# A fused transformer block's attention: one more merging transfer and one more addition in place of two raw chunks, a ring of nine slots, and the batch loop written out

## The reference, cut to what matters

```python
x = x + 0.5 * ffn(layernorm(x))
x = x + attn(layernorm(x))
x = x + 0.5 * ffn(layernorm(x))

def attn(x, Uq, Vq, bq, Uk, Vk, bk, Uv, Vv, bv):      # H = 8 heads of 32 columns
    q, k, v = lowrank(x, Uq, Vq, bq), lowrank(x, Uk, Vk, bk), lowrank(x, Uv, Vv, bv)
    scores = einsum('bqhd,bkhd->bhqk', q, k) / 32 ** 0.5
    out = einsum('bhqk,bkhd->bqhd', softmax(scores), v)
```

## Time and profile before

| | us |
|---|---|
| median of 3 runs | 4593.1 (4589.04 to 4593.98) |
| the profiled execution | 4578.01, with a span of 4576.3 |
| ACT, exponentials of scores (L1674) | 2256.0 busy, 4096 of them |
| POOL, additions to a running sum (L1537) | 1771.0 busy, 633.5 idle before them |
| PE, scores (L1795) | 1535.0 busy, 4096 of them |
| merging transfers (L1514) | 384 of 1024 KB, 8.4 from issue to landing |

### The profile page before, as it was taken

How to read it: one execution, slowest core, us unless ns; L and a number is a source line. 1 busy time by engine, 2 the same in 40 slices (tenths; PEclk the granted TensorE clock), 3 DMA queues, 4 the chain that set the end, 5 groups by cost and what they waited for, 6 DMA issues and landing times. The chain is left out here.

```text
span 4576.3 us, 72040 instructions
## 1 busy us (share of the span) xinstructions
PE 3734.0 (82%) x21202; PEld 1454.5 (32%) x21202; DVE 3267.3 (71%) x4504; ACT 3214.1 (70%) x6587; POOL 2553.1 (56%) x966
## 2 busy tenths in 40 slices
PE   0177683899999999999999999999999999920276
PEld 0144452233333333333333333333333333300143
DVE  8644675887777777777777777777777777648544
ACT  5043572788888888878888887888888888834043
POOL 0011001477777777767777777777777777753111
PEclk9988896899999999999999999999999999965588
DMA  8200899577877878778777887788788788678100
GB/s 276 77 3 4 293 392 293 106 158 160 174 168 164 170 169 179 158 159 173 166 162 166 174 177 153 171 168 176 160 177 168 158 175 166 129 226 300 37 5 5
DMA packets 326047, 743.31 MB, mean 162 GB/s; under 512 B 26060, under 2 KB 209888, under 8 KB 270112
## 3 DMA queue, kind: packets, MB, share of 16 engines
q0 software_dynamic: 57216, 407.92, 44.8%
q1 hardware_dynamic: 222496, 284.46, 20.9%
q10 hardware_dynamic: 45952, 46.27, 2.9%
HBM read 198.90 MB, written 136.48 MB: 73 GB/s over the span
## 5 line engine op out<-in xcount | busy, mean ns | idle before, releaser
L1674 ACT ACTIVATE at_probs<-at_ps_s 128x512 f32<-128x512 f32 x4096 | 2256.0, 613 | 345.6 <-PE at_ps_s L1795 261.6
L1559 DVE TENSOR_REDUCE at_part_max<-at_ps_max 128x3 f32<-128x1536 f32 x1024 | 1801.0, 1759 | 472.4 <-PE at_ps_max L1708 464.5
L1537 POOL TENSOR_TENSOR at_pool_sum<-at_pool_sum,at_probs 128x2048 f32<-128x2048 f32 x384 | 1771.0, 4612 | 633.5 <-DMA at_probs<-at_probs 632.4
L1795 PE MATMUL at_ps_s<-at_qs,at_ks 97*128 97x512 f32 (+1 forms) x4096 | 1535.0, 453 | 37.2 <-ACT at_probs L1674 22.5
L1742 PE MATMUL at_ps_acc<-at_probs,at_v 128*32 128x512 f32 x8192 | 1099.2, 609 | 0.9 <-ACT at_probs L1674 0.9
L1795 PEld LDWEIGHTS at_ps_s<-at_qs,at_ks 97*128 97x128 f32 (+1 forms) x4096 | 630.4, 189 | 1149.2 <-ACT at_probs L1674 823.0
L1561 DVE TENSOR_REDUCE at_part_max<-at_max_copy 128x1 f32<-128x512 f32 x1024 | 691.7, 676 | 0.0
L1623 ACT COPY at_max_copy<-at_ps_max 128x512 f32<-128x512 f32 x1024 | 610.1, 596 | 102.1 <-PE at_ps_max L1708 101.8
L1708 PE MATMUL at_ps_max<-at_ks,at_qs 32*128 32x512 f32 x4096 | 526.0, 501 | 82.5 <-DMA at_ks<-qk_parts 48.8
L1514 POOL DMA_DIRECT2D at_probs<-at_probs x384 | 346.9, 903 | 209.1 <-PE at_ps_acc L1742 201.3
L1708 PEld LDWEIGHTS at_ps_max<-at_ks,at_qs 32*128 32x128 f32 x4096 | 197.9, 183 | 439.7 <-issue 381.3
(11 more groups left out here) (195 smaller groups left out, 2705.5 us busy)
## 6 DMA issues: line engine op xcount, KB each, us to landing
at_probs<-at_probs POOLq DMA_DIRECT2D x384, 1024.0 KB, 8.4
qk_parts<-pr_hi SPq DMA_DIRECT2D x32, 1024.0 KB, 12.1
qk_parts<-pr_lo SPq DMA_DIRECT2D x32, 1024.0 KB, 12.3
at_qs<-qk_parts SPq DMA_DIRECT2D x320, 64.0 KB, 6.0
at_ks<-qk_parts SPq DMA_DIRECT2D x80, 256.0 KB
s_x<-in_x SPq DMA_DIRECT2D x16, 1024.0 KB
after_ffn<-s_y ACTq DMA_DIRECT2D x16, 1024.0 KB, 6.6
v_tokens<-pr_v SPq DMA_DIRECT2D x32, 512.0 KB, 10.9
```

Source lines behind the costliest of these rows:

```text
L1537: nc.gpsimd.tensor_tensor(acc, a, probs[:, c % RING], ALU.add).then_inc(pool_added, 1)
L1559: nc.vector.reduce_max(part_max[:, 0:HG - 1, t, c], ps_max[:, 0:HG - 1], AX.X).then_inc(three_max_done, 1)
L1674: nc.scalar.activation(probs[:, c % RING, h], ps_s[:, BANK[j]], ACT.Exp, scale=SCALE).then_inc(exp_done, 1)
L1795: nc.tensor.matmul(ps_s[:, BANK[j]], ks[rows, g, h, c * P:(c + 1) * P], qs[rows, un % NQB, h, :], start=True, stop=True).then_inc(scores, 1)
```

## The change

The chunks 14 and 15 become a seventh merged pair. The merge now adds the second slot of a pair into the first, so POOL's chunks are 0, 1, 2, 4, ... 14, with eight additions; a merge is issued when the first slot has been multiplied and the second's exponentials are done. The closing moves to cycle 6 and the turning of the output to cycle 7, and the closing's raw matmuls go. POOL's list alternates an issue and an addition, and the last two additions of a unit stand in the next unit's list. The ring has nine slots, which a unit doesn't divide, so slots and banks are worked out for all 64 units and the loop over batch pairs is written out on all engines. The bank for the closing is the oldest of the three and no fixed one. To make room, q has three buffers and is loaded two units ahead. Up to four merges may be out (`MERGES_OUT`).

```diff
-RAW_CHUNKS = (14, 15)
-DMA_PAIRS = ((2, 3), (4, 5), (6, 7), (8, 9), (10, 11), (12, 13))
-DMA_BEFORE_ADD = (1, 1, 2, 3, 4, 5)
-POOL_CHUNKS = (0, 1, 3, 5, 7, 9, 11, 13)
-CLOSE_IN = 5
-NORM_IN = 6
+DMA_PAIRS = ((2, 3), (4, 5), (6, 7), (8, 9), (10, 11), (12, 13), (14, 15))
+POOL_CHUNKS = (0, 1, 2, 4, 6, 8, 10, 12, 14)
+CLOSE_IN = 6
+NORM_IN = 7
...
+def score_banks(units, tiles, per_cyc):
+    order, last, bank, after = list(range(RINGS)), {}, {}, {}
+    def use(user, k):
+        bank[user], after[user], last[k] = k, last.get(k), user
+    def take(user):
+        k = order.pop(0)
+        order.append(k)
+        use(user, k)
+    take((-1, "m"))
+    for unit in range(units):
+        for j in range(tiles):
+            if unit > 0 and j == CLOSE_IN * per_cyc + 2:
+                use((unit, "z"), order.pop(0))
+            if unit > 0 and j == (NORM_IN + 1) * per_cyc + 2:
+                order.insert(0, bank[unit, "z"])
+            take((unit, j))
+            if unit + 1 < units and j == TURN_MAX_IN * per_cyc + 1:
+                take((unit, "m"))
+    use((units, "z"), order[0])
+    return bank, after
...
-    RING = 8
-    NQB = 4
+    RING = 9
+    NQB = 3
+    MERGES_OUT = 4
...
+    def slot(unit, c):
+        return (unit * NC + c) % RING
...
-                    if un + 3 < BU or not last:
+                    if un + 2 < BU or not last:
                         sp.wait_ge(scores, unit * TILES)
                         sp.sem_inc(load_turn, 1)
-                        load_q(b + (un + 3) // BU, (un + 3) % BU)
+                        load_q(b + (un + 2) // BU, (un + 2) % BU)
...
+            def start_pair(unit, d):
+                a, c = DMA_PAIRS[d]
+                pool.wait_ge(pv_done, unit * NC + a + 1)
+                pool.wait_ge(exp_done, unit * TILES + c * HG + HG)
+                pool.sem_inc(dma_turn, 1)
+                nc.gpsimd.dma_start(probs[:, slot(unit, a)], probs[:, slot(unit, c)], accum_op=ALU.add
+                                    ).then_inc(dma_added[(unit * ND + d) % MERGES_OUT], 16)
...
+            for unit in range(B * BU):
+                if unit > 0:
+                    add(unit - 1, ADDS - 2)
+                start_pair(unit, 0)
+                if unit > 0:
+                    add(unit - 1, ADDS - 1)
+                start_pair(unit, 1)
+                for d in range(2, ND):
+                    add(unit, d - 2)
+                    start_pair(unit, d)
+                add(unit, ND - 2)
+            for n in (ADDS - 2, ADDS - 1):
+                add(B * BU - 1, n)
...
-                        for c in RAW_CHUNKS:
-                            for h in range(HG):
-                                nc.tensor.matmul(ps_close[h * DH:(h + 1) * DH, :], ones[:, 0:DH], probs[:, c % RING, h],
-                                                 start=(c == RAW_CHUNKS[0]), stop=False)
                         pe.wait_ge(pool_added, n * ADDS + ADDS)
...
-            with pe.Fori(0, B // 2 - 1) as pair:
-                batch(pair * 2 + 1)
-                batch(pair * 2 + 2)
+            for b in range(1, B - 1):
+                batch(b)
```

More of the change, by code:

```diff
@@ L1374, in attend @@
         pool_added = sem("pool_added")
-        dma_added = [sem(f"dma_added{n}") for n in range(2)]
+        dma_added = [sem(f"dma_added{n}") for n in range(MERGES_OUT)]
         dma_turn = sem("dma_turn")
@@ L1428, in row_of_max @@
                     to = SHIFT_AT[first]
-                    sp.dma_start(qs[to:to + 1, un % NQB, first:end].bitcast(F32)
+                    sp.dma_start(qs[to:to + 1, unit % NQB, first:end].bitcast(F32)
                                  .rearrange("a h (t q) -> a (h t) q", q=P),
@@ L1444, in _ @@
             load_kv(0, 1)
-            load_q(0, 2)
             row_of_max(0, 0)
@@ L1503, in _ @@
                 nc.gpsimd.memset(ks[to:to + 1, :, first:end].bitcast(F32), 1.0).then_inc(ones_row, 1)
[L1505 to L1537, removed]
@@ new lines, in add @@
+            def add(unit, n):
+                acc = pool_sum[:, unit % 2]
+                c = pool_chunks[n + 1]
+                paired = [d for d in range(ND) if DMA_PAIRS[d][0] == c]
+                if paired:
+                    k = unit * ND + paired[0]
+                    pool.wait_ge(dma_added[k % MERGES_OUT], (k // MERGES_OUT + 1) * 16)
+                else:
+                    pool.wait_ge(exp_done, unit * TILES + c * HG + HG)
+                if n == 0:
+                    if unit > 1:
+                        pool.wait_ge(z_done, unit - 1)
+                    first = probs[:, slot(unit, pool_chunks[0])]
+                else:
+                    pool.wait_ge(pool_added, unit * ADDS + n)
+                    first = acc
+                nc.gpsimd.tensor_tensor(acc, first, probs[:, slot(unit, c)], ALU.add).then_inc(pool_added, 1)
@@ L1609, in _ @@
             batch(0, first_batch=True)
-            with dve.Fori(0, B // 2 - 1) as pair:
-                batch(pair * 2 + 1)
-                batch(pair * 2 + 2)
+            for b in range(1, B - 1):
+                batch(b)
             batch(B - 1, last=True)
@@ L1673, in batch @@
                         act.wait_ge(scores, unit * TILES + j + 1)
-                        nc.scalar.activation(probs[:, c % RING, h], ps_s[:, BANK[j]], ACT.Exp, scale=SCALE
+                        nc.scalar.activation(probs[:, slot(unit, c), h], ps_s[:, BANK[unit, j]], ACT.Exp, scale=SCALE
                                              ).then_inc(exp_done, 1)
@@ L1690, in _ @@
             batch(0, first_batch=True)
-            with act.Fori(0, B // 2 - 1) as pair:
-                batch(pair * 2 + 1)
-                batch(pair * 2 + 2)
+            for b in range(1, B - 1):
+                batch(b)
             batch(B - 1, last=True)
@@ L1707, in scores_for_max, with after_last, turn_max @@
                     rows = slice(HI_AT[h], HI_AT[h] + DH)
-                    last = nc.tensor.matmul(ps_max[:, h], qs[rows, un % NQB, h, t * P:(t + 1) * P],
+                    last = nc.tensor.matmul(ps_max[:, h], qs[rows, unit % NQB, h, t * P:(t + 1) * P],
                                             ks[rows, un % BU // NU, h, c * 512:(c + 1) * 512], start=True, stop=True)
                 last.then_inc(max_scores, 1)
-            def turn_max(unit, bank):
+            def after_last(unit, w):
+                if AFTER[unit, w] is None:
+                    return
+                before, x = AFTER[unit, w]
+                if x == "z":
+                    pe.wait_ge(o_done, before)
+                elif x == "m":
+                    pe.wait_ge(max_row_done, before + 2)
+                else:
+                    pe.wait_ge(exp_done, before * TILES + x + 1)
+            def turn_max(unit):
                 pe.wait_ge(neg_max_done, unit + 1)
-                nc.tensor.transpose(ps_s[0:HG * QT, bank, 0:P], neg_max[:], ident[:]).then_inc(max_turned, 1)
+                nc.tensor.transpose(ps_s[0:HG * QT, BANK[unit - 1, "m"], 0:P], neg_max[:], ident[:]).then_inc(max_turned, 1)
             pe.wait_ge(consts, 2)
@@ L1793, in score @@
                         rows = slice(0, LAST_ROW[h])
-                        after_last(j)
-                        nc.tensor.matmul(ps_s[:, BANK[j]], ks[rows, g, h, c * P:(c + 1) * P], qs[rows, un % NQB, h, :],
+                        after_last(unit, j)
+                        nc.tensor.matmul(ps_s[:, BANK[unit, j]], ks[rows, g, h, c * P:(c + 1) * P], qs[rows, unit % NQB, h, :],
                                          start=True, stop=True).then_inc(scores, 1)
```

98 lines of the change are left out of this document (28 added, 70 removed).

## The result

| | before | after |
|---|---|---|
| median, us | 4593.5 (4589.0 to 4599.0, 4 runs) | 4376.5 (4373.8 to 4379.6, 4 runs) |
| ratio | | 0.9527 (0.9511 to 0.9544) |
| span of the profiled execution | 4576.3 | 4373.6 |

What follows compares the result with a forecast made beforehand. Bound: a loop through PE and ACT, plus lateness. 63 x (46.70 + 0.55 - 50.16) = -183, +5 for the tail: -178, so 4400 us profiled, plus 15 carried over: 4415 us; forecast 4380 to 4440 (0.55), range 4375 to 4505.

Steps and rivals of the forecast that it cites:

- Raw chunks gone, 1.74 us a unit: Closing cycle on PE: dropping 16 matmul records shortens it from 6.07 to 4.33 us, -110 us over 63 units.
- The lateness of 91 us: Units' delay over a clean unit, 1.45 us each, from late merges and POOL additions; claimed to go, save a small allowance.
- 1.8 us inside the new deadline: Last merge of a unit: may land as late as 12.5 us after issue; the average of 10.7 is in time.
- What was left of lateness, 0.55 us a unit: Allowance per unit: 0.2 us at the close, 0.15 in slots, 0.1 for the row of maxima, 0.1 for the rest.
- The DMA engines at 97%: Seven merges plus SP's queue take 45.2 us of a 46.7 us unit, as an upper bound.
- Rival 1: DMA engines become the bound: unit 48.2 us with 3 us idle, 4475 us; chance 0.26 together with a second rival.
- The row of maxima: Small transfer needed by a unit's first score: 6.4 us without cost, missed more often, 0.1 us a unit.
- Rival 3: Row of maxima waits behind merges: 4497 us, or 4831; mild form or another rival 0.09, slower kernel 0.08.
- Written out, -17 us: Loop over batch pairs: writing it out removes PE's two stops at the loop's end, 17 us together.
- The tail, +5: After the last attention matmuls: issue and three additions make the close come after 14.6 us instead of 9.8, +5 us.
- The median 15 us above the profiled execution: Runs' median 4593.1 against profiled 4578.0 us; the 15 us were carried over, making 4400 into 4415 us.
- The pace is set by this loop: Normal 2.76 us cycle: attention matmuls wait for exponentials, which wait for scores; PE work inside lengthens it one to one.

## Why the prediction was right, point by point

**Raw chunks gone, 1.74 us a unit:** right. 1.75 in the closing cycle, 1.69 in the mean unit when the same work is put back, 1.60 when the raw chunks are.

**The lateness of 91 us:** right that it goes, wrong why, so this part of the number was in part luck; and what was left over was mis-sized. The step from the average landing of 10.7 us to "1.8 us inside the new deadline" took the landing of the last merge as given and asked only what waits for it. The runs with the ring of nine show that the deadline isn't it: move it by one cycle and POOL's list is later by most of it. What shortens the list is that two additions stand between an issue and the addition of its result. The prediction had this as a remark ("it may land 11 us after issue") and gave it no share; and its "before, it came after one" misread the old list, in which the first merge of a unit has none. The two runs with raw chunks, nine slots and the close in cycle 6 take 4621 us with the old list and 4472 with the new, and differ in little but that. The earlier issue of a merge and its direction differ as well and were not tried alone. The trace leaves little to the first: with the old list and the late close POOL waited for PE 32 us in all, under 0.6 us a unit, of 2.12 between the two runs.

**What was left of lateness, 0.55 us a unit:** measured 46.81 - 46.69 = 0.12. That is 27 of the 38 us between forecast and result; another 14 are the 15 us carried over (below), and 2 went the other way.

**The DMA engines at 97%:** measured 96.3%, a merge 77.9% x 2000 / 300 = 5.19 us. Rival 1 put 3 us of idle engines on top; measured are 3.7% of 46.81, 1.7 us. The sign "merges take over 12 us to land" came in 18 of 435 (the longest 13.7) and cost next to nothing, for the list leaves nearly that long.

**The row of maxima:** 0.3 us in all. Rival 3 didn't happen: the last packets of the row ended at most 4.8 us after issue. In six of 63 units two merges were out when the row was issued, and even there it took no more than 4.4 us, so it didn't wait for both. The rule of turns by whole packets that the prediction weighed (the Trainium skill, "DMA: Bandwidth & Descriptors", section "Queues, rings and completion order") is neither shown nor refuted by this.

**Written out, -17 us:** 16 by the traces, 30 by the runs.

**The tail, +5:** +5.1, by luck. From the last attention matmuls to the close it was to grow from 9.8 to 14.6 us and grew to 16.6, +6.8: POOL issued its last merge 1.1 us behind those matmuls and began the three additions 0.9 us later. Against that stands that the raw matmuls also left the closing that falls into the last unit, 1.7 us that the 63 units of the sum don't hold.

**The median 15 us above the profiled execution:** wrong. After the change it is 1.4. With the measured terms the sum for the profiled execution is 63 x (46.81 - 50.16) + 5.1 = -206, and it became 203 us shorter; the medians show 217.

**"The pace is set by this loop" through PE and ACT:** imprecise. In the changed trace PE's list has no gap in a normal cycle of 2.76 us. In the last unit, where PE has no maxima to compute, PE stands idle in each cycle and the cycle takes 2.67 us: that is the loop's own length, so in all other units it is PE's own work that counts. The sum didn't hang on it, for both lengthen one to one.

## What to carry to other kernels

An engine that issues a transfer, and later uses its result in the same in-order list, needs enough own work between the two to cover the landing; count the length of that list with its waits, and compare it with the period before asking which deadline is missed. Price a short stop of PE from a run or row in which it happens: here 2.4 us of stopping cost 4.7 a unit. Where a stage ends in a chain on one engine while another is idle, its last piece can be done differently from all others: it gave 14.5 us here.

## What the runs showed of the hardware that was not expected

PE's stops of 2 to 4 us in or just ahead of the closing had stretches at half clock behind them in nearly every unit (55 and 47 between 850 and 3700 us in two runs, 3.4 to 10.2 us long), while the changed kernel, in which the longest wait of PE for POOL before the last unit was 1.2 us, had none. In the run with the close in cycle 5, they cost about as much as the stops: 4.7 us a unit, of which 2.4 are the stop. The DMA engines ran at 96 to 99% of their time over the 2 ms read, with 1 MB merges still landing in 8.5 to 8.8 us (median). The packets of a transfer of 1 MB from memory to memory took 2.5 us of the sixteen engines, a merge of 1 MB within SBUF 5.2. And at 99% it is the small pieces on the other queue that come late, not the merges: the last piece of k took 12.7 us where it had taken 5.5.
